# A four-layer transformer kernel on one core: the second layer's attention batch by batch, its preparation interleaved with the work around it

## The reference

```
layer 0:  x = x + s * silu(FFN(xn) + xn)     # 8 experts, top 2, one shared expert; s = attention output
layer 1:  xn = layernorm(x)
          q, k = rope(rms_norm(xn Wq)), rope(rms_norm(xn Wk))   # 16 query heads, 4 key heads of 16
          s = softmax(q k^T / 4) v Wo                           # not causal
          then 8 routed experts (top 2) and a shared expert
layer 2:  attention with 16 causal heads of 128, FFN with 1024 hidden columns (gelu)
layer 3:  the same in shape, FFN with ternary weights and 4-bit activations
```

## Time and profile before

| | us |
|---|---|
| median of 3 runs | 1367.53 (1365.57 to 1368.49) |
| the profiled execution: its own time | 1368.73 |
| its span | 1366.9 |
| PE busy | 1236.5 (90%) |
| DVE busy | 725.4 (53%) |
| ACT busy | 612.5 (45%) |
| POOL busy | 122.4 (9%) |
| mean granted PE clock | 0.966 of full |

### The profile page before, as it was taken

The page is one execution under the profiler, slowest core; times in us unless marked ns, Lnnn a source line. Parts: engine busy times, 40 slices in busy tenths (PEclk is TensorE's granted clock), DMA queues, the critical chain, the costliest instruction groups (busy, mean ns, idle before and its releaser), DMA issues.

```text
span 1366.9 us, 18855 instructions
## 1 busy us (share of the span) xinstructions
PE 1236.5 (90%) x6396; PEld 777.1 (57%) x6396; DVE 725.4 (53%) x2019; ACT 612.5 (45%) x1518; POOL 122.4 (9%) x144
## 2 busy tenths in 40 slices
PE   5888888759999979999999899799999999999994
PEld 4644444452276545656565687566666666667853
DVE  3776525563143378787878710344344444446357
ACT  2635443369922224545455402345454444442053
POOL 3320012344000300000000000000000000000000
PEclk9979999869999989999999999899999999999998
DMA  8001100501122400000000002100000000000000
GB/s 243 1 18 41 33 27 0 168 5 59 36 77 92 182 12 12 12 12 13 8 8 8 1 1 73 66 21 15 24 13 24 13 24 12 24 12 1 1 0 31
DMA packets 28046, 48.64 MB, mean 36 GB/s; under 512 B 3903, under 2 KB 22303, under 8 KB 26887
## 3 DMA queue, kind: packets, MB, share of 16 engines
q1 hardware_dynamic: 25222, 38.13, 8.6%
q0 software_dynamic: 2736, 9.37, 2.3%
HBM read 40.36 MB, written 9.19 MB: 36 GB/s over the span
## 4 chain that ended last, share of the span: by engine, by line
PE 68%; DVE 13%; issue 10%; ACT 4%; POOL 3%; DMA 1%; SPq 0%; ACTq 0%; POOLq 0%; DVEq 0%
PE bank L890 13%; PE bank L906 9%; PE bank L897 8%; PE bank L883 5%; PE bank L875 5%; PE bank L901 4%; PE bank L779 4%; PE bank L763 3%; PE bank L1110 2%; PE bank L1072 2%; PE bank L1205 2%; PE bank L1128 1%; ACT PT L1349 1%; PE bank L1191 1%; PE bank L734 1%
## 5 line engine op out<-in xcount | busy, mean ns | idle before, releaser
L1235 ACT COPY R<-bank 128x512 f32<-128x512 f32 (+4 forms) x203 | 110.5, 560 | 324.6 <-PE bank L906 142.8
L1870 DVE CUSTOM_DVE_ANT_0 bank<-bank,mask_row 128x128 f32<-128x128 f32 (+3 forms) x256 | 127.0, 497 | 173.4 <-PE bank L897 170.9
L890 PE MATMUL bank<-XNT,W 128*128 128x512 f32 x416 | 203.7, 614 | 6.9 <-ACT R L1235 3.8
L1374 ACT ACTIVATE R<-bank,nm 128x128 f32<-128x128 f32 (+3 forms) x256 | 136.2, 532 | 109.3 <-DVE nm L1870 108.4
L890 PEld LDWEIGHTS bank<-XNT,W 128*128 128x128 f32 x416 | 76.4, 194 | 103.3 <-issue 95.2
L897 PE MATMUL bank<-R 128*128 128x512 f32 (+3 forms) x384 | 134.3, 434 | 0.0
L1349 ACT ACTIVATE PT<-bank 128x512 f32<-128x512 f32 (+3 forms) x256 | 110.0, 520 | 41.3 <-PE bank L768 37.9
L875 PE MATMUL bank<-W,R 128*128 128x256 f32 x576 | 125.3, 380 | 3.2 <-ACT R L1235 3.2
L875 PEld LDWEIGHTS bank<-W,R 128*128 128x128 f32 x576 | 109.1, 190 | 18.7 <-ACT R L1235 2.1
L901 PE MATMUL bank<-identf,R 128*128 128x128 f32 x640 | 112.4, 275 | 6.4 <-DVE R L1887 4.7
L906 PE MATMUL bank<-PT,R 128*128 128x128 f32 (+3 forms) x384 | 112.0, 435 | 5.6 <-ACT PT L1235 4.3
(11 more groups left out here) (256 smaller groups left out, 1768.6 us busy)
## 6 DMA issues: line engine op xcount, KB each, us to landing
W<-in_wq SPq DMA_DIRECT2D x32, 128.0 KB, 2.0
W<-in_wo SPq DMA_DIRECT2D x2, 2048.0 KB, 11.7
W<-in_egu SPq DMA_DIRECT2D x1, 2816.0 KB
W<-in_wk SPq DMA_DIRECT2D x20, 128.0 KB, 2.1
W<-in_wv SPq DMA_DIRECT2D x20, 128.0 KB, 2.0
R<-xg SPq DMA_DIRECT2D x5, 512.0 KB, 4.5
yg<-R SPq DMA_DIRECT2D x5, 512.0 KB, 3.1
W<-in_wa SPq DMA_DIRECT2D x2, 1024.0 KB, 5.1
```

Of the source, the lines that this page charges most:

```text
L890: ins = mm(bank[:, :], wqkv23[:, s, c, :], XNT[:, c, b * SEQ:(b + 1) * SEQ], start=c == 0, stop=c == DC - 1)
L1235: return nc.scalar.copy(dst, src)
L1374: return fn(Pr[c][:, 0:n], PS[c][:, 0:n], ACT.Exp, scale=-1.0, bias=nm[:, c:c + 1], accum_out=esum[:, c:c + 1])
L1870: return dve.tensor_tensor_reduce(out=s[:, 0:n], in0=s[:, 0:n], in1=mask_row[:, SEQ - n:SEQ], scale=-1.0, scalar=-MASKED, op0=ALU.add, op1 ...
```

## The change

Four things change; what is computed stays the same.

- **Layer 0's FFN.** Batch 1's first four chunks are made between batch 0's four down products. Batch 0's norm for layer 1, its transposes, projections, `take` and `rotate` stand among batch 1's later chunks; its four stacks among batch 1's four down products. silu is made as sigmoid on ACT and one more multiplication on DVE. The hidden tiles of batch 1 get memory of their own.
- **Layer 1's attention** goes through batch 0's four units first, then batch 1's. Batch 1's norm, projections, router and stacks stand inside batch 0's 16 steps. The scores rotate over three banks (0, 1, 2); banks 3, 5 and 7 serve the inserted work. The scattering moves to units 5 to 7.
- **Layer 2's FFN** is written out instead of looped; batch 0's norm for layer 3 and its transposes stand among batch 1's chunks.
- **Layer 3's attention** projects batch 0 at once and does batch 1's norm and transposes after batch 0's first four scores.

The diff, cut to its core:

```
...
+        def stack1_banks(m):
+            return [3 * (m % 2) + k for k in range(3)] if m < TPB else [3, 5, 7]
+        def projection_bank(m):
+            return 6 + m % 2 if m < TPB else (3, 7)[m % 2]
+        def turn_bank(l, k):
+            return k if l == 0 else (6, 7, 3, 7)[k] if l == 1 else 2 + k if l == 3 else k
...
-        ORDER0 = (0, 1, 2, 3, 11, 4, 5, 6, 7, 8, 12, 9, 10)
+        ORDER0 = (0, 1, 2, 3, 4, 5, 11, 6, 7, 8, 12, 9, 10)
...
-        SCORE_BANK, OUT_BANK, TURN_BANK = ((0, 1, 2), (0, 1, 2, 5)), 4, 6
+        OUT_BANK, TURN_BANK = 4, 6
...
-        SCATTER_AT = {1: (0, 1), 2: (2, 3), 3: (4, 5), 4: (6, 7)}
+        SCATTER_AT = {5: (0, 1, 2), 6: (3, 4, 5), 7: (6, 7)}
...
-                        n, banks = (g * stages + w) * GH + h, SCORE_BANK[l]
-                        pe.wait_ge(cb["pb_ready"], n + 1 + GH - len(banks))
...
+            def attention1():
...
+                def scores(s):
+                    u, j = s // TPB, s % TPB
+                    b, g = u // NG, u % NG
+                    if g == 0 and j == 0:
+                        pe.wait_ge(stk_act, 2 * NT + TPB)
+                        pe.wait_ge(stk_dve, 2 * NT + STACKS_A + STACKS_B * b)
+                    for h in range(GH):
+                        n = s * GH + h
+                        pe.wait_ge(cb["pb_ready"], n + 1 + GH - 3)
+                        ins = mm(PS[n % 3][:, :], kstk[0:KQ, g, b * SEQ + j * P:b * SEQ + (j + 1) * P],
+                                 qstk[0:KQ, g * GH + h, b * SEQ:(b + 1) * SEQ], start=True, stop=True)
+                        ins.then_inc(cb["st_ps"], 1)
+                def values(s):
+                    u, j = s // TPB, s % TPB
+                    if j == 0:
+                        pe.wait_ge(cb["vs_ready"], u + 1)
+                        pe.wait_ge(cb["oe_ready"], u + 1)
+                    pe.wait_ge(cb["pb_ready"], (s + 1) * GH + GH)
+                    for h in range(GH):
+                        ins = mm(PS[OUT_BANK][32 * h:32 * h + 32, :], vs[u % 2][:, j, 0, :],
+                                 PT[:, s % 2, h, :], start=j == 0, stop=j == TPB - 1)
+                    ins.then_inc(cb["pv_ps"], 1)
...
+                scores(0)
+                for s in range(UNITS1 * TPB):
+                    if s + 1 < UNITS1 * TPB:
+                        scores(s + 1)
+                    if s % TPB == 0 and s > 0:
+                        turn_outputs(s // TPB - 1)
+                    values(s)
+                    if s == 3:
+                        ln_transpose(1, (2, 3))
+                    elif s == 4:
+                        project1(4)
+                        project1(5)
+                    elif s == 5:
+                        project1(6)
+                    elif s == 6:
+                        project1(7)
+                    elif s in (10, 11, 12, 13):
+                        stack1_transpose(s - 6)
+                    elif s == 15:
+                        ranks()
+                turn_outputs(UNITS1 - 1)
...
+                for n in range(NCH):
+                    gate_up(0, n)
+                for t in range(TPB):
+                    down(t)
+                    gate_up(1, t)
+                for n in range(TPB, NCH):
+                    gate_up(1, n)
+                    if n == 8:
+                        ln_transpose(1, (0, 1))
+                    elif n == 9:
+                        for m in range(TPB):
+                            project1(m)
+                down(4)
+                down(5)
+                stack1_transpose(0)
+                down(6)
+                stack1_transpose(1)
+                down(7)
+                stack1_transpose(2)
+                stack1_transpose(3)
...
-                pe.wait_ge(xnt_ready, LN_PAIRS * 4)
+                pe.wait_ge(ffn[2]["f"], NT)
                 k = 0
                 for b in range(B):
+                    if b == 1:
+                        ln_transpose(3, (2, 3))
+                    pe.wait_ge(xnt_ready, LN_PAIRS * 3 + 2 * b + 2)
...
+                        if b == 1 and m == 5:
+                            ln_transpose(3, (0, 1))
...
+            def attention1():
+                cb = coreb[1]
+                act.sem_inc(cb["pb_ready"], 4)
+                for s in range(UNITS1 * TPB):
+                    act.wait_ge(cb["pv_ps"], s + 1)
+                    for h in range(GH):
+                        n = s * GH + h
+                        act.wait_ge(cb["st_ps"], n + 1)
+                        fn(PT[:, s % 2, h, :], PS[n % 3][:, :], ACT.Exp, scale=HD ** -0.5).then_inc(cb["pb_ready"], 1)
+                    if s == 4:
+                        ln_copy(1, (2, 3))
+                    elif s == 5:
+                        take(4)
+                        take(5)
+                    elif s == 6:
+                        take(6)
+                    elif s == 7:
+                        take(7)
+                    elif s == 8:
+                        router_act(1)
+                    elif s in (9, 10, 11, 12):
+                        stack1_first(s - 5)
...
+                def post(tile):
+                    act.wait_ge(f["f"], tile + 1)
+                    if tile >= 2:
+                        act.wait_ge(f["xup"], tile - 1)
+                    fn(gpost0[tile % 2], fpost0[tile % 2], ACT.Sigmoid).then_inc(f["g"], 1)
+                for t in range(TPB):
+                    post(t)
+                    gate(1, t)
+                for n in range(TPB, NCH):
+                    gate(1, n)
+                    if n == 8:
+                        ln_copy(1, (0, 1))
+                    elif n == 9:
+                        for m in range(TPB):
+                            take(m)
+                stack1_first(0)
+                stack1_first(1)
+                post(4)
+                post(5)
+                stack1_first(2)
+                stack1_copy(0)
+                post(6)
+                stack1_first(3)
+                stack1_copy(1)
+                post(7)
+                stack1_copy(2)
+                stack1_copy(3)
...
+            def attention1():
+                def norm(u):
+                    normalise(1, u, u // NG, u % NG)
+                store_outputs(1, 0)
+                norm(0)
+                rotate(4)
+                rotate(5)
+                rotate(6)
+                store_outputs(1, 1)
+                rotate(7)
+                router(1)
+                norm(1)
+                probabilities(1)
+                largest(0)
+                stack1_rest(4)
+                stack1_last(4)
+                stack1_rest(5)
+                stack1_copies(4)
+                stack1_last(5)
+                store_outputs(1, 2)
+                stack1_copies(5)
+                stack1_rest(6)
+                norm(2)
+                stack1_last(6)
+                stack1_rest(7)
+                stack1_copies(6)
+                stack1_last(7)
+                stack1_copies(7)
+                largest(1)
+                chosen()
+                store_outputs(1, 3)
+                slots()
+                norm(3)
+                for u in range(NG, UNITS1):
+                    store_outputs(1, u)
+                    norm(u)
...
                 def update(tile):
+                    g = gpost0[tile % 2]
                     dve.wait_ge(f["g"], tile + 1)
-                    own(tt(gpost[tile % 2], gpost[tile % 2], S[:, tile, :], ALU.mult))
-                    tt(X[:, tile, :], X[:, tile, :], gpost[tile % 2], ALU.add).then_inc(f["xup"], 1)
+                    own(tt(g, g, fpost0[tile % 2], ALU.mult))
+                    own(tt(g, g, S[:, tile, :], ALU.mult))
+                    tt(X[:, tile, :], X[:, tile, :], g, ALU.add).then_inc(f["xup"], 1)
...
+                for n in range(NCH):
+                    hidden(0, n)
+                for t in range(TPB):
+                    tail(t)
+                    if t >= 1:
+                        update(t - 1)
+                    if t == TPB - 1:
+                        update(t)
+                    hidden(1, t)
+                dve.wait_ge(f["xup"], TPB)
+                ln_stats(1, 0)
+                hidden(1, 4)
+                hidden(1, 5)
+                ln_scale(1, 0)
+                for n in range(6, 10):
+                    hidden(1, n)
+                for m in range(TPB):
+                    rotate(m)
+                for n in range(10, NCH):
+                    hidden(1, n)
+                dve.sem_inc(coreb[1]["oe_ready"], 1)
+                dve.sem_inc(coreb[1]["otok_done"], 2)
+                stack1_rest(0)
+                tail(4)
+                stack1_last(0)
+                stack1_rest(1)
+                tail(5)
+                update(4)
+                stack1_last(1)
+                stack1_copies(0)
+                stack1_rest(2)
+                update(5)
+                tail(6)
+                stack1_last(2)
+                stack1_copies(1)
```

(23 more changed lines are left out.)

## The result

| | us | ratio to before |
|---|---|---|
| before | 1368.01 median of 4 | |
| changed | 1355.92 median of 4 (1353.62 to 1357.94) | 0.9911 [0.9884, 0.9938] |
| changed, second measurement | 1356.64 (before: 1365.28) | 0.9941 [0.9920, 0.9961] |
| changed, third measurement | 1355.33 (before: 1366.49) | 0.9927 [0.9902, 0.9952] |

The change takes 12.1, 8.6 and 11.2 us off. The prediction was 1351.0 with a range of 1338 to 1362: direction and range held, and the time lies 5 us above it. The profiled execution took 1354.29 us, with a span of 1352.5; before it was 1366.9, so the spans differ by 14.4 us, where the prediction's sum has 16.5. Of the 5 us, 2.1 are therefore in the sum.

A forecast was written before the change was run, and what follows sets the result against it. PE, busy 90% of the span, was taken to bound the kernel, but ACT in layer 1's attention. The terms -39.6, +31.1 and -8 gave -16.5, so a median of 1351.0 us, range 1338 to 1362.

The forecast's parts named there:

- Part 1: From layer 0's first down product to layer 1's first scores: scores start 39.6 us earlier, at least 32, at most 43.
- the 3 us added for slips between four engines: Before layer 1's first scores: 3 us allowed for waits between engines handing stacks on and for a clock that may fall.
- Part 2: Layer 1's attention, exponentials from first to last: 97.9 us against 66.8, so +31.1.
- The ring: Layer 1's attention: with three banks, exponential, freed score, values and next scores make 2.46 us per step, not 1.97.
- A turned unit: Layer 1's attention: seven transposes of a finished unit lie between its steps, 0.6 us each, 4.2 in all.
- insertions: Layer 1's attention: inserted norm, projections, router, stacks and ranks cost 15.4 us; ACT's take operations fit within the steps.
- Part 3: Layer 2's end to layer 3's first turned tile: 8.6 us less, taken as -8, bounds -4 and -10.
- the bound of -4: Layer 2 to layer 3: the gain is only 4 us if the clock still falls there.
- The free third bank: Rival, layer 1's attention: three banks cost nothing, 1.97 us per step stays, 1334 us; chance 0.10.
- The stacks in series: Rival, layer 1's attention: inserted stacks run one after another, four cost 15.5 us; 1361; chance 0.17 including a late start.
- The clock did not stay down in attention: Rival, layer 1's attention: half clock for batch 0's 16 steps, +35 us, 1386, slower than before; chance 0.07.
- the rule that the prediction quotes: Start of layer 1's attention: transposes don't count as PE work, so clock 1.2 GHz, about 4 us slower in all.

The follow-up runs named there:

- its own experiment: Kernel before the change with three score banks (0, 1, 2) in place of four for layer 1's attention; 1380.47 us, ratio 1.0116.
- the last experiment above: Changed kernel with batch 0's four stacks behind all four last down products of layer 0, not among them; 1363.40 us, ratio 0.9983.

## Why the prediction came out as it did

- **What bounds the kernel.** Right in the place, not quite in the engine. In layer 1's attention of before, ACT was busy for 64.9 of 68 us and PE for 66.5: four scores (0.97) and the values (1.00) make the same 1.97 as four exponentials. Both were full, which is why any wait between them shows at once.
- **Part 1, -39.6: measured -40.7.** Two errors cancel, which is luck. PE's projections began at 237.16 in place of 234.8 and the last product came 2.7 us later than summed. The large chunk at 230.02 waited 3.56 us for the product at 229.28, and DVE had the updates of two tiles in front of that one:

```profile
226.24 1.38 DVE L2153 TENSOR_TENSOR R<-R 128x256 f32<-128x256 f32 x1
227.65 1.26 DVE L2154 TENSOR_TENSOR R<-R 128x256 f32<-128x256 f32 x1
...
229.28 0.68 DVE L2170 TENSOR_TENSOR W<-R,bank 128x512 bf16<-128x512 f32 x1
```

  Two of these operations took 1.38 and 1.26 us where the sum had 0.43; why is not shown. In return the 3 us added for slips between four engines weren't needed.
- **Part 2, +31.1: measured +36.5. The mechanism holds; this is the part whose size was wrong, and in it the term for the insertions.** The ring is exact: 2.46. A turned unit adds 0.44, not 0.60, so 3.1 for 4.2. The term "insertions", 15.4, is what is left of 102.4: 102.4 - 76.3 - 3.1 - 2.0 = 21.0. By steps over 2.46 it splits into the two first steps at half clock 0.4, norm's transposes 1.2 (0.9 predicted), takes and projections 7.8 (5.3), the router 2.0 (2.4), stacks 9.3 (6.3), the ranks 0.4 (0.5). I had let ACT's take "stay under" the ring, and a stack's first parts likewise in the steps in which PE turns a stack, because ACT had the time for them. But they stood ahead of the exponential that the ring needs, and the take can't start before PE's projection lands. The first parts of tiles 6 and 7 waited besides (1.34 and 1.35 us) for the transposes that free their buffers. About 0.9 of the stacks' 9.3 is the half clock at 303.5 (values in 1.92 for 1.06), which follows the router's wait. Moving the insertions behind that exponential gave 7.3 us back, more than the 5.5 by which these two terms were too small, since it also shortened the router's steps. ACT's table for the exponential was loaded behind the first score, 0.9 later than before, and that was not in the sum.
- **Part 3, -8: measured -9.2 in the traces, -4.5 and -5.0 between medians.** The clock at full speed behind the new order's seam came true in eight of nine profiles (in the ninth the stretch took 18.6). By the medians the part is worth only a little over half of the 8, near the bound of -4, but not for that bound's reason: the new order keeps its clock, and the old one perhaps loses less in executions without a profile. This is not shown.
- **The rivals.** The free third bank is refuted by its own experiment. The stacks in series came true in half of its mechanism: not a chain of the stacks alone, but each inserted piece in series with the ring, and it cost 5.5 us, not 9. Its sign, steps 8 to 13 of over 5 us with PE waiting for DVE, did not show: they took 3.3 to 4.8, and PE waited for ACT, but for one wait of 0.47. The clock did not stay down in attention: 1.00 from 276 to 303 and from 327 on, 0.93 between.
- **Transposes and the clock.** In the kernel before, PE has nothing but transposes from 281.71 to 306:

```profile
276.00:280.30 4.30, 0.00 (x0) 0.00 (x0) 1.78 (x5) 4.30 (x19) 2.00 (x4) 1.00 0.00 0
280.50:304.20 23.70, 15.47 (x134) 14.39 (x135) 19.54 (x49) 15.55 (x31) 12.63 (x23) 0.50 0.00 1
304.40:306.00 1.60, 1.49 (x27) 1.34 (x24) 1.31 (x3) 1.22 (x2) 0.00 (x0) 1.00 0.00 0
```

  So the 0.61 of the earlier trace rows was a mixture: the lower level for 24 us, and the upper one at both ends. The middle looks like the rule that the prediction quotes; the ends speak against it. The clock fell at 280.4, ahead of the first transpose, while PE stood still in a wait of 5.89 us, and it came back at 304.3 behind transposes alone, the 60 that run packed from 300.36. In the last experiment above it also fell in a wait and came back at 265.4 behind forty packed transposes. Not every packed group did that: forty from 294.69 to 299.43 did not. So transposes alone can bring the clock back here, and what preceded each of these falls is a PE that stood still; whether transposes count for less than products is not shown. In the change the transposes between down products ran at 1.00. The price was overestimated too: the two first steps lost 0.4 us to the clock, not 4, since it was back by 272.8.

## What to carry to other kernels

When two engines hand buffers round in a circle, sum the links once through: if the sum is over the work of the busier engine, the buffer count sets the pace, and each thing inserted ahead of the link that closes the circle is paid in full even on an engine with time to spare. Put inserted work behind the instruction that the other engine waits for, and take a spare buffer as soon as it is free, if only for some of the steps. Before one instruction of a group is moved by itself, ask whether the group's time was shared by instructions running side by side.

## What the runs showed of the hardware that was not expected

- Four products of 128 rows by 32 columns, on four groups of columns, take 1.07 us; one of them alone takes 1.05.
- Transposes alone brought the clock back from 0.50 to 1.00, at 304.3 in the kernel before and at 265.4 in the one with the stacks behind the down products.
- The same instructions, ahead of anything an edit touched, got another clock in another execution. In ten profiles of kernels with the same code there, the first exponential of layer 1 started between 266.1 and 271.1. From batch 0's second large chunk to that exponential it took 61.4 to 62.2 us in the five in which the clock stood at 1.00 from 225 to 240, and 62.9 to 65.2 in the five that had 0.77 to 0.89 there. Differences of up to 4 us between single executions can come from that alone, and between the change's three measurements, medians of four to six, the gain still differed by 3.5.
